# Row sums of the softmax one group later, and the context matmuls ahead of them

## The reference

```python
def _L1_attn_ref(hidden_states, Wq, bq, Wk, bk, Wv, bv):
    NUM_HEADS = 16; HEAD_DIM = 64
    q = heads(_int_linear(hidden_states, Wq, bq))
    k = heads(_int_linear(hidden_states, Wk, bk))
    v = heads(_int_linear(hidden_states, Wv, bv))
    scores = jnp.einsum('bhqd,bhkd->bhqk', q, k) / np.sqrt(hd)
    probs = jax.nn.softmax(scores, axis=-1)
    ctx = jnp.einsum('bhqk,bhkd->bhqd', probs, v)
...
# --- layer 1 ---
xn = _layernorm(x); s = _L1_attn_ref(xn, ...); g = _silu(_L1_ffn_ref(xn, ...))
x = x + s * g
```

## Time and profile before

| | us |
|---|---|
| two timed runs | 7044.56 and 6605.07, median 6824.81 |
| the profiled execution | 6609.82 |
| span of its slowest core (core 2) | 6608.3 |
| spans of the eight cores | 6572.3 to 6608.3 |
| TensorE busy | 5271.3 (80% of the span) |
| ScalarE busy | 1705.6 (26%) |
| VectorE busy | 1186.4 (18%) |
| mean granted clock of TensorE, core 2 | 0.872 |

### The profile page before, as it was taken

The page is one execution under the profiler, slowest core; times in us unless marked ns, Lnnn a source line. Parts: engine busy times, 40 slices in busy tenths (PEclk is TensorE's granted clock), DMA queues, the critical chain, the costliest instruction groups (busy, mean ns, idle before and its releaser), DMA issues.

```text
span 6608.3 us, 62008 instructions; the slowest of 8 cores (6572.3 to 6608.3 us)
## 1 busy us (share of the span) xinstructions
PE 5271.3 (80%) x23769; PEld 2109.6 (32%) x24088; DVE 1186.4 (18%) x1753; ACT 1705.6 (26%) x2153; POOL 361.9 (5%) x679
## 2 busy tenths in 40 slices
PE   6676777665677761677777776999999999999999
PEld 3322222222222220222222221444444444444444
DVE  4312000140111226322223232100100010001000
ACT  0143677501011110344444444100110011011001
POOL 0000000001000000000000000200110011002000
PEclk7777899888899985677777887999999999999999
DMA  4000000005534334000000000999998999889998
GB/s 116 3 11 1 13 7 7 13 19 114 135 105 106 103 107 153 26 1 1 1 1 1 1 1 17 162 155 151 160 159 151 152 160 161 151 151 163 159 151 142
DMA packets 153489, 560.09 MB, mean 85 GB/s; under 512 B 16754, under 2 KB 21106, under 8 KB 112244
## 3 DMA queue, kind: packets, MB, share of 16 engines
q0 software_dynamic: 99920, 417.38, 38.1%
q1 hardware_dynamic: 53284, 138.72, 6.7%
HBM read 927.24 MB, written 33.55 MB: 145 GB/s over the span
## 4 chain that ended last, share of the span: by engine, by line
PE 68%; ACT 8%; DVE 8%; DMA 8%; issue 7%; DVEq 1%; ACTq 0%; SPq 0%; POOL 0%; POOLq 0%
PE pb L1463 13%; PE pb L1481 13%; PE pb L1499 3%; PE psA L544 3%; PE psA L1436 3%; PE psA L1441 3%; ACT pt L611 3%; PE psA L1331 2%; DVE sqrot L1383 2%; PE psA L876 2%; PE pb L1349 2%; PE pb L1211 2%; PE psA L1151 2%; ACT pt L608 2%; PE psA L926 1%
## 5 line engine op out<-in xcount | busy, mean ns | idle before, releaser
L1463 PE MATMUL pb<-hA,wHb 128*128 128x512 bf16 x4014 | 882.1, 380 | 12.2 <-DVE hA L1450 7.9
L1481 PE MATMUL pb<-hB,wHb 128*128 128x512 bf16 x4014 | 880.4, 379 | 8.8 <-ACT hB L1469 4.5
L1463 PEld LDWEIGHTS pb<-hA,wHb 128*128 128x128 bf16 x4096 | 400.9, 98 | 493.4 <-issue 11.9
L1481 PEld LDWEIGHTS pb<-hB,wHb 128*128 128x128 bf16 x4096 | 400.5, 98 | 488.7 <-issue 6.3
L1331 PE MATMUL psA<-q_p,k_p 64*128 64x512 bf16 x1024 | 290.6, 449 | 107.7 <-ACT pt L1357 70.3
L1512 DVE TENSOR_TENSOR sg<-gt,smix 128x512 f32<-128x512 bf16 x32 | 22.2, 692 | 1964.3 <-ACT gt L1506 1927.9
L876 PE MATMUL psA<-xng,w1hb 128*128 128x512 bf16 x1004 | 260.0, 406 | 141.7 <-DMA w1hb<-w1ht 56.8
L581 PE MATMUL psA<-q_p,k_p 64*128 64x512 bf16 x1024 | 221.2, 444 | 133.3 <-ACT pt L611 81.4
L1383 DVE RECIPROCAL sqrot<-sqrot 1x1024 f32<-1x1024 f32 x32 | 209.3, 6541 | 625.3 <-ACT sqrot L1381 625.3
L1357 ACT ACTIVATE pt<-psA,col_tmpa 128x1024 bf16<-128x1024 f32 x256 | 284.5, 1111 | 123.9 <-PE psA L1331 121.8
L1487 ACT ACTIVATE hA<-pb,vcol 128x512 bf16<-128x512 f32 x128 | 88.0, 687 | 801.2 <-PE pb L1481 801.2
(11 more groups left out here) (319 smaller groups left out, 5203.8 us busy)
## 6 DMA issues: line engine op xcount, KB each, us to landing
wHb<-h1wt POOLq DMA_DIRECT2D x128, 1024.0 KB, 10.9
wHb<-h2wt POOLq DMA_DIRECT2D x128, 1024.0 KB, 10.2
w12b<-w1wt POOLq DMA_DIRECT2D x128, 256.0 KB, 5.4
w12b<-w2wt POOLq DMA_DIRECT2D x128, 256.0 KB, 6.5
wHb<-w3wt POOLq DMA_DIRECT2D x32, 1024.0 KB, 10.6
w1hb<-w1hS SPq DMA_DIRECT2D x96, 256.0 KB, 2.7
w2hb<-w2hS SPq DMA_DIRECT2D x48, 512.0 KB, 3.4
xrot<-xT SPq DMA_DIRECT2D x16, 1024.0 KB, 6.4
```

What stands on the lines that cost most here:

```text
L1463: emitter(lambda t, it=it, slh=slh, bank=bank: t.matmul(psB[bank][:, :], wslH[slh][:, it, :], hA[:, it, :], start=(it == 0), stop=(it == 31)))
L1481: emitter(lambda t, it=it, slh=slh, bank=bank: t.matmul(psB[bank][:, :], wslH[slh][:, it, :], hB[:, it, :], start=(it == 0), stop=(it == 31)))
```

## The change

In the loop the row sums go from two groups behind the scores to three, and stand behind the context matmuls of the group. The context of group 0 is issued at group 2 without the wait for the copies of the spread reciprocals; that wait goes to group 3, ahead of the row sums of group 0. The tail has the context of groups 6 and 7 first, then the row sums of groups 5, 6 and 7, so twelve matmuls where there were eight. The last row sum of each four in the loop and the last of the tail raise the counter ct, and pt2_mm, by which the exponentials know that a slot is free, is set behind the row sums.

```diff
--- before.py
+++ after.py
@@ -1340,18 +1340,24 @@
                         if grp == 2:
                             if pend[0] is not None:
                                 emit_norm()
+                            wt("t", cv, aev.get(("ctx", par), 0))
+                        emit_ctx(pgrp, psl, par)
+                        pt2_mm[psl] = ct.n
+                    if grp >= 3:
+                        rgrp = grp - 3
+                        rsl = rgrp % 4
+                        if grp == 3:
                             wt("t", cs, sc2_ev.get("rb", 0))
-                            wt("t", cv, aev.get(("ctx", par), 0))
                         for h in range(2):
                             for tkk in range(2):
-                                tk = 2 * pgrp + tkk
+                                tk = 2 * rgrp + tkk
                                 off = (2 * h + tkk) * 512
-                                TN(lambda t, tk=tk, psl=psl, off=off, h=h: t.matmul(
+                                emitter = TI if (h == 1 and tkk == 1) else TN
+                                emitter(lambda t, tk=tk, psl=rsl, off=off, h=h: t.matmul(
                                     psB[4 + h][0:1, 0:512], onesc_bf[:],
                                     pt2[:, psl, off:off + 512],
                                     start=(tk == 0), stop=(tk == NTT - 1)))
-                        emit_ctx(pgrp, psl, par)
-                        pt2_mm[psl] = ct.n
+                        pt2_mm[rsl] = ct.n
                     wt("s", ct, t_half[0])
                     wt("s", ct, pt2_mm.get(ptsl, 0))
                     sc2_ev["A"] = SI(lambda s, ptsl=ptsl: s.activation(
@@ -1363,19 +1369,20 @@
                         bias=col["tmpa"][:, 5:6], scale=0.125))
                 wt("t", cs, sc2_ev["B"])
                 for pgrp in (6, 7):
+                    emit_ctx(pgrp, pgrp % 4, par)
+                for pgrp in (5, 6, 7):
                     psl = pgrp % 4
                     for h in range(2):
                         for tkk in range(2):
                             tk = 2 * pgrp + tkk
                             off = (2 * h + tkk) * 512
-                            TN(lambda t, tk=tk, psl=psl, off=off, h=h: t.matmul(
+                            emitter = TI if (pgrp == 7 and h == 1 and tkk == 1) else TN
+                            emitter(lambda t, tk=tk, psl=psl, off=off, h=h: t.matmul(
                                 psB[4 + h][0:1, 0:512], onesc_bf[:],
                                 pt2[:, psl, off:off + 512],
                                 start=(tk == 0), stop=(tk == NTT - 1)))
-                for pgrp in (6, 7):
-                    emit_ctx(pgrp, pgrp % 4, par)
                 t_ctx = ct.n
-                pt2_mm[2] = pt2_mm[3] = t_ctx
+                pt2_mm[1] = pt2_mm[2] = pt2_mm[3] = t_ctx
                 wt("s", ct, t_ctx)
                 SN(lambda s: s.copy(sqrot[1][0:1, 0:512], psB[4][0:1, 0:512]))
                 s_rs = SI(lambda s: s.copy(sqrot[1][0:1, 512:1024], psB[5][0:1, 0:512]))
```

## The result

The changed kernel is slower by 0.8%: 1.0084 times the time of the kernel before, with a 95% interval of 1.0042 to 1.0126. Some executions of either kernel are lengthened by a few per cent by a disturbance that is not the kernel's, so the medians over all runs (6770.1 before, 6712.25 after) don't compare them; undisturbed, before took 6605 to 6617 us and after 6652 to 6661. The profiled executions stand at 6609.82 and 6660.65 us.

A forecast was written before the change was run, and what follows sets the result against it. Each attention block was taken as bound by its chain of tail, reciprocal, copies and TensorE-ScalarE alternation. 32 blocks x (0.86 tail - 0.60 loop gain) = +8 us on 6609.82, so 6618 us; range 6588 to 6655.

The forecast's parts named there:

- I expect the rise about 1 us later than now: Group 3: TensorE's granted clock returns to full at 2955.2 in the block read, because its unbroken run begins later.
- the term worked out from it: Loop part of a block: last exponentials come 0.75 us sooner, taken as a gain of 0.6 us a block.
- The tail: Block's end: four more row sums that nothing hides delay ScalarE's copies and the reciprocal by 0.86 us a block.
- The wait filled, A(3) sooner: Group 2: context runs under ScalarE's copies, filling TensorE's 1.52 us wait; group 3's exponentials start 1.8 us sooner.
- TensorE gives it back at group 3: Group 3: context and group 0's row sums at half clock nearly give back the 1.8 us before group 4's scores.
- The clock: Group 3: TensorE's unbroken run begins at 2951.1 instead of 2950.08, so its clock rises about 1 us later.
- The bound for it: Loop, clock low into group 4: up to 0.7 us more at half rate, a loss of 0.3 us a block.
- Seams: Rival: context before row sums costs 0.1 us in each of about 6 groups, 6637 us, chance 0.14; the sum took 0.
- a period over 33.3: Sign of a wrong forecast: reciprocals over 33.3 us apart would mean the new order costs at its seams.
- Early clock: Rival: spreading plus group 0's context, one 4.8 us run, lifts the clock early; net 0.94 us a block, 6580 us, chance 0.11.
- Nothing outside the attention: Stages before and after layer 1's attention: no change; any change there would show the forecast wrong.
- The place to look: Layer 1's attention, slices 17 to 25, some 1,380 us: called the one place where reordering TensorE's work could pay.

The follow-up runs named there:

- after_pair: Changed kernel, but group 3's scores of both heads wait for the second head's exponentials of group 2; period 33.69 us, shortest execution 6643 us.
- loop_only: Changed kernel, but group 7 does the row sums of groups 4 and 5, leaving eight in the tail; period 33.07 us, shortest execution 6622 us.
- ctx_first: Kernel before, with context ahead of row sums in loop and tail, the copies' wait between them at group 2, no group shift; period 31.31 us, shortest 6569 us.
- row_fill_again: Kernel before plus 4, 1 and 6 unread one-partition matmuls behind the scores of groups 0, 1, 2; second run; period 33.11 us, shortest 6646 us.
- hot_before: Kernel before plus 4, 1 and 6 unread 128 x 512 matmuls behind the scores of groups 0, 1, 2; period 30.60 us, shortest 6587 us.
- tail_only: Kernel before, with only group 5's row sums moved to the tail, which then does twelve; period 34.11 us, shortest execution 6663 us.

## Why the prediction was wrong

I forecast 6618 us, +0.3 us a block; it is 6660.65, +1.53, outside the range of 6588 to 6655, though within the 2% that I held nearly certain. The step that failed is the sentence "I expect the rise about 1 us later than now" and the term worked out from it.

- *The tail, 0.86 a block:* right, 0.85 measured.
- *The wait filled, A(3) sooner:* right. A(2) to A(3) was put at 2.4 and is 2.42; B(3) is 1.7 sooner.
- *TensorE gives it back at group 3:* right as mechanism, and S(4) at half clock was put at 17.72 us after the reciprocal (2955.85), where it is measured.
- *The clock:* wrong. I took the unbroken run to begin at S(3), because TensorE is busy from there on, and let the rise move with it by 1 us. It came 4.0 us later than before: the half-clock stretch itself grew, from 13.7 us to 17.1 in 184 of 192 blocks, and C(2) and R(1) of group 4 were at half clock too. So the term was a loss of 0.67 and not a gain of 0.60: 1.27 us, 41 us over 32 blocks, all but 2 us of the miss. The rest of the sum was sound: in the seven blocks in which the rise came at 17.2, some 1 us late as forecast, A(7) is at 25.42 on the average, 0.54 sooner than before, where I had 0.6. Why the run from S(3) on did not end the stretch in time stays open. One head after the other is not it alone, since with S(3) in pairs (after_pair) the stretch is as long.
- *The bound for it:* too near. "Up to 0.7 more" gave A(7) at most 26.3 us after the reciprocal; it is 26.86 in the block shown, because more lay at half clock than I allowed.
- *Seams:* rightly taken as 0, as loop_only and ctx_first show. That rival's 6637 was nearer the result than my forecast, for a reason that isn't there; and I had named a period over 33.3 as the sign of it, a sign that the clock gives as well.
- *Early clock:* the opposite happened. The Trainium skill, TensorE: Matmul & The Clock Gate, section on the clock gate, has activity release the throttle; the spreading and C(0) in one run of 4.7 us (the row at 3182.41 in the block above, to 3187.15, where the wait of 1.55 begins) did not release it, and row_fill_again shows that one-row work didn't hold it either.
- *Nothing outside the attention:* right, 49 of 50.8 us lie in the blocks.
- *The place to look:* I called this stage the one place where reordering TensorE's work could pay. The earlier trace rows do not say that: slices 1 to 14 have TensorE 5 to 7 tenths busy too. Nothing in the sum hangs on it.

## What to carry to other kernels

When work is moved out of the place where an engine warms up, its price is not its duration but where the clock rises afterwards; take as the bound a clock that stays low through the next group as well. Moving work behind a wait and deferring it by a stage are two edits: here the first alone gains 0.6%, and both together lose 0.8%. When two halves of a change are run apart, compare the parts of the block and not only its length: a change at the end of one block can move the clock in the next. And before a stretch counts as keeping TensorE's clock up, look at how many rows its matmuls use.

## What I had not expected of the hardware

- bf16 matmuls of one row keep TensorE busy and didn't hold its clock, where the same count with 128 rows did: A(2) at 12.43 against 10.04 us, period 33.11 against 30.60.
- The fp32 spreading takes 2.0 us at full clock (hot_before) and 3.75 at half, so it follows the clock; whether it holds it, no run shows apart from the pause behind it.
- With a pause of 1.85 us ahead of the tail the clock fell within the tail, and that cost 1.7 us there (4.37 us for twelve row sums instead of 2.69; 109 of 192 blocks of tail_only). With 0.91 to 1.58 us it didn't fall.
- Six useless full-height matmuls in the critical stretch, 2.23 us in the block shown, shortened the block by 1.0 us.
